# Transformer layer with routed experts: weight parts split by GpSimd within the attention, last shared block placed behind the expert tiles, padding rows copied at the end

## The reference

```
x = x + attn(layernorm(x))          # 16 query heads of 16, 4 key/value heads, causal softmax,
                                    # ternary weights for q, k, v and for the projection
h = layernorm(x)
scores = sigmoid(h @ w_router)      # 8 experts, the best 2 of each token, weights normalised
for e in range(8):
    he = silu(h @ w1[e]) * (h @ w3[e])              # 256 -> 176
    out = out + combine[:, e:e+1] * (he @ w2[e])    # 176 -> 256
shared = silu(h @ ws1) * (h @ ws3) @ ws2            # 256 -> 352 -> 256
x = x + out + shared
```

## Time and profile before

| | |
|---|---|
| median of 3 runs | 584.66 us (582.53 to 585.18) |
| profiled execution | 584.15 us, of which the span from the first to the last instruction is 582.2 us |
| mean granted TensorE clock | 0.915 of full speed |
| busy | TensorE 474.1 us, ScalarE 362.3, VectorE 313.5, GpSimd 170.9 |
| transfers | 61.36 MB, mean 105 GB/s |

### The profile page before, as it was taken

One profiled execution on the slowest core, in us unless ns is written; L12 is line 12 of the kernel. 1 busy time (PEld: TensorE's weight loads), 2 busy tenths in 40 slices (PEclk: granted clock), 3 DMA queues, 4 the chain that ended last, 5 costly groups with the idle time before them and its releaser, 6 DMA issues.

```text
span 582.2 us, 9830 instructions
## 1 busy us (share of the span) xinstructions
PE 474.1 (81%) x3202; PEld 264.9 (45%) x3202; DVE 313.5 (54%) x886; ACT 362.3 (62%) x567; POOL 170.9 (29%) x222
## 2 busy tenths in 40 slices
PE   1694869999999999999398768859797889999930
PEld 1582323233333333333143424327675789998920
DVE  6973516834713156131276555535957567666726
ACT  4255759989999989998369556615242335555520
POOL 3721101011110220103241172044455824444430
PEclk9878969999999999999599987868899989999985
DMA  8111012963999469243521022211011434444349
GB/s 207 31 48 41 11 32 86 301 163 98 289 296 282 112 48 4 1 92 98 145 55 57 2 74 86 62 43 56 28 57 40 124 74 119 124 117 125 110 138 340
DMA packets 77525, 61.36 MB, mean 105 GB/s; under 512 B 26984, under 2 KB 70600, under 8 KB 77480
## 3 DMA queue, kind: packets, MB, share of 16 engines
q1 hardware_dynamic: 73784, 51.04, 36.7%
q0 software_dynamic: 3408, 9.34, 4.5%
q10 hardware_dynamic: 288, 0.39, 0.2%
HBM read 19.88 MB, written 29.34 MB: 85 GB/s over the span
## 4 chain that ended last, share of the span: by engine, by line
PE 48%; DVE 18%; issue 14%; DMA 5%; POOL 5%; ACT 5%; SPq 4%; another core or an unknown queue 1%; DVEq 0%; ACTq 0%; POOLq 0%
PE ps L1575 16%; PE ps L1555 10%; PE ps L1747 6%; ACT prob L783 4%; PE ps L1765 3%; POOL rows_by_expert L658 2%; SPq L369 2%; PE ps L1584 2%; PE ps L1495 2%; DVE sm L922 2%; DMA yfin<-pair_out 2%; DVE sm L921 2%; PE ps L1769 1%; POOL hid_lo L687 1%; PE ps L1516 1%
## 5 line engine op out<-in xcount | busy, mean ns | idle before, releaser
L783 ACT ACTIVATE prob<-ps 128x1024 f32<-128x1024 f32 (+3 forms) x320 | 260.1, 919 | 70.6 <-PE ps L1555 68.6
L1575 PE MATMUL ps<-prob,v_sb 128*32 128x512 f32 (+3 forms) x1280 | 158.3, 569 | 18.3 <-DVE o_sb L1073 9.6
L1555 PE MATMUL ps<-qk 64*128 64x512 f32 (+3 forms) x640 | 121.1, 442 | 20.4 <-DMA qk<-qT 12.3
L617 POOL TENSOR_SCALAR_AFFINE_SELECT prob<-prob 128x512 f32<-128x512 f32 x64 | 41.3, 647 | 228.3 <-ACT prob L783 227.3
L1555 PEld LDWEIGHTS ps<-qk 64*128 64x128 f32 x640 | 54.1, 192 | 114.5 <-ACT prob L783 82.2
L1575 PEld LDWEIGHTS ps<-prob,v_sb 128*32 128x32 f32 x1280 | 26.0, 110 | 64.7 <-issue 34.0
L719 POOL DMA_INDIRECT pair_out<-yo,xg x39 | 37.5, 963 | 54.7 <-DVE yo L1431 54.4
L1073 DVE COPY o_sb<-ps 128x512 f32<-128x512 f32 x16 | 11.1, 691 | 65.2 <-PE ps L1575 64.6
L1693 PE MATMUL ps<-x2T,ws_hi 128*128 128x512 f32 (+1 forms) x96 | 33.0, 427 | 4.4 <-DVE hid L1300 4.4
L658 POOL DMA_INDIRECT rows_by_expert<-xs,slots x32 | 31.4, 981 | 14.2 <-issue 8.7
L1060 DVE CAST qT<-ps 96x512 fp32r<-96x512 f32 x16 | 11.0, 686 | 36.8 <-PE ps L1516 36.8
(11 more groups left out here) (203 smaller groups left out, 782.0 us busy)
## 6 DMA issues: line engine op xcount, KB each, us to landing
rows_by_expert<-pads SPq DMA_DIRECT2D x9, 1935.0 KB, 19.8
qk<-qT SPq DMA_DIRECT2D x138, 64.0 KB, 2.1
xg<-rows_by_expert SPq DMA_DIRECT2D x39, 129.0 KB
yfin<-pair_out SPq DMA_DIRECT2D x8, 512.0 KB, 7.3
stage<-in_w SPq DMA_DIRECT2D x8, 352.0 KB
x_sb<-in_x SPq DMA_DIRECT2D x4, 512.0 KB, 7.3
qk<-shT SPq DMA_DIRECT2D x8, 256.0 KB, 4.8
res<-in_x SPq DMA_DIRECT2D x4, 512.0 KB, 4.2
```

Of the source, the lines that this page charges most:

```text
L617: nc.gpsimd.affine_select(out=t, in_=t, compare_op=ALU.is_ge, fill=0.0, base=0, pattern=[[0, HPG], [1, P]], channel_multiplier=-1).then_in ...
L783: nc.scalar.activation(prob[:, u % NPB, 2 * hf:2 * hf + 2, c0:CH], ps[:, b:b + 2, c0:CH], ACT.Exp, scale=SCALE).then_inc(exp_done, 1)
L1555: ins = M(ps[:, 2 * (n % NSB) + h, c0:CH], qk[rows, par, PAIRS, kt * P:(kt + 1) * P], qk[rows, par, hf, j * CH + c0:(j + 1) * CH], start=T ...
L1575: ins = M(ps[VW * h:VW * (h + 1), O_BANK, c0:CH], v_sb[:, kt, :], prob[:, u % NPB, h, c0:CH], start=(kt == 0), stop=(u == LAST_OF[j]), ski ...
```

## The change

- Raw pieces are loaded during groups 0 to 2 into `NRAW` = 3 buffers, and GpSimd makes both parts into `NSPLIT` = 3 buffers, between masks in groups 1 and 2 (`SPLIT_AT`: behind unit 3, 11 and 23, 2 to 5 pieces at a place). SyncE stores the parts to DRAM and loads them back whole in the last group (`ws`, `ws2`, `w13`) and behind it (`w2_parts`). `high_piece` and `low_piece` are gone. The GpSimd loop over groups is written out.
- An expert's segment has 128 rows more (`SEG`). Only one block of 15 x 128 padding rows is written in DRAM (`pads_d`); when the last place is known, SyncE copies 128 of them behind each expert's last row (8 copies at run-time rows), and waits for these before it loads tiles.
- The last shared block's `up(11)` and `down(9..11)` are issued behind the tiles; its eviction stands between the second and the third of the four final additions.
- `hid_lo` of units 4 to 11 is made by VectorE; VectorE's order in the shared stage changes (`choose(2)` behind `scale_x2(3)`, `take_shared(1)` behind `list_tiles`), steps of `AFTER` move, step (4, 2) goes from unit 37 to 39.
- In group 0 round 1 is turned before the attention, rounds 2 and 3 one and two units earlier, and the scores of units 4 and 5 come behind the product of unit 3.

```diff
-SHARED_PIECES, EARLY_PIECES, POOL_PIECES = KD + 1, 9, 15
...
-NST = 2
-RES_AFTER = {4: 1, 7: 2, 8: 3}
+NRAW, NSPLIT = 3, 3
...
-    0: [("round", 0, 1)], 4: [("out", 0, 0)], 8: [("round", 0, 2)], 12: [("out", 0, 1)], 16: [("round", 0, 3)],
+    7: [("round", 0, 2)], 8: [("out", 0, 0)], 12: [("out", 0, 1)], 14: [("round", 0, 3)],
...
-    (0, 0): [("out", 0, 3), ("step", 5, 2)], (1, 0): [("step", 6, 2), ("step", 0, 3), ("step", 1, 3)],
-    (2, 0): [("step", 2, 3)], (2, 1): [("step", 3, 3)], (3, 0): [("step", 7, 2)],
-    (5, 0): [("step", 4, 3), ("step", 5, 3)], (6, 0): [("step", 6, 3)], (7, 1): [("step", 7, 3)],
+    (0, 0): [("out", 0, 3), ("step", 5, 2)], (1, 0): [("step", 0, 3), ("step", 1, 3), ("step", 6, 2)],
+    (2, 0): [("step", 2, 3), ("step", 3, 3)], (4, 0): [("step", 4, 3), ("step", 5, 3)],
+    (5, 0): [("step", 7, 2), ("step", 6, 3)], (6, 1): [("step", 7, 3)],
...
-LATE_PIECE_AT = {1: 9, 2: 10, 3: 11, 4: 12, 5: 13, 6: 14, 8: 15, 9: 16, 11: 17, 12: 18}
 EXP_AT = {19: 0, 31: 1}
-EXP_AFTER = {1: 2, 6: 3}
-LOW_PIECES = {3: range(0, 3), 11: range(3, 5), 23: range(5, EARLY_PIECES)}
+SPLIT_AT = {(1, 3): 2, (1, 11): 4, (1, 23): 3, (2, 3): 2, (2, 11): 5, (2, 23): 3}
+FLAT_FIRST = (NC - 1) * SH
+LOW_ON_DVE = range(4, FLAT)
...
+            def load_raw(n):
+
+                if n >= NRAW:
+                    sp.wait_ge(split_done, n - NRAW + 1)
+                for r, at, shape, src, _ in pieces_of(n):
+                    sp.dma_start(shaped(raw[0:r, n % NRAW, at:at + size_of(shape)], shape), src
+                                 ).then_inc(ld_raw[n % NRAW], 16)
+
+            def store_parts(n):
+
+                sp.wait_ge(split_done, n + 1)
+                for r, at, shape, _, to in pieces_of(n):
+                    for part in range(2):
+                        sp.dma_start(to[part], shaped(parts_f[0:r, n % NSPLIT, part, at:at + size_of(shape)], shape)
+                                     ).then_inc(st_parts[n % NSPLIT], 16)
+
+            def next_pieces(n0, n1):
+
+                for n in range(n0, n1):
+                    store_parts(n)
+                    if n + NRAW < len(PIECES):
+                        load_raw(n + NRAW)
...
+            for n in range(NRAW):
+                load_raw(n)
             sp.wait_ge(consts, CONSTS)
-            clear_rows(0, 3)
+            sp.dma_start(pads_d.rearrange("(k p) c -> p k c", p=P), pads[:].broadcast_to([P, PADS, ROW])).then_inc(zeroed, 16)
             for c in range(NC):
                 move(1, c)
-            sp.wait_ge(s_ready, 2 * NU)
-            clear_rows(3, blocks)
+            sp.wait_ge(zeroed, 16)
+            sp.dma_start(pads_d[:, ID:ID + 1].rearrange("(k p) c -> p k c", p=P), pad_ids[:].bitcast(F32),
+                         allow_slow_non_contiguous=True).then_inc(padded, 16)
+            next_pieces(0, 6)
             for c in range(NC):
                 move(2, c)
-            sp.wait_ge(zeroed, 16 * blocks)
-            for b in range(blocks):
-                sp.dma_start(rows_d[b * PADS * P:(b + 1) * PADS * P, ID:ID + 1].rearrange("(k p) c -> p k c", p=P),
-                             pad_ids[:, b * PADS:(b + 1) * PADS, :].bitcast(F32),
-                             allow_slow_non_contiguous=True).then_inc(padded, 16)
+            next_pieces(6, 9)
+            sp.wait_ge(padded, 16)
+            sp.dma_start(rows_d[E * SEG:ROWS, :], pads_d[E * P:PADS * P, :]).then_inc(padded, 16)
+            next_pieces(9, 16)
             for c in range(NC):
                 move(3, c)
+            next_pieces(16, len(PIECES))
+            for b in range(NSPLIT):
+                sp.wait_ge(st_parts[b], parts_stored(max(range(b, len(PIECES), NSPLIT))))
...
+            sp.dma_start(ws[:].bitcast(F32), ws_d).then_inc(ld_ws, 16)
+            sp.dma_start(ws2[:].bitcast(F32)[:, :, 0:SH - 1], ws2_d[:, :, 0:SH - 1]).then_inc(ld_ws, 16)
...
+            sp.wait_ge(x_free, step_use(3, 0))
+            sp.dma_start(res[:], x_t[:, TPC:2 * TPC, :]).then_inc(ld_res, 16)
+            for part in range(2):
+                sp.dma_start(w13[:, part].bitcast(F32), w13_d[:, part]).then_inc(ld_w13, 16)
+            for j in range(2, NC):
+                sp.wait_ge(x_free, step_use(3, j - 1))
+                sp.dma_start(res[:], x_t[:, j * TPC:(j + 1) * TPC, :]).then_inc(ld_res, 16)
+            sp.wait_ge(pv_done, NPB + NU * NKV)
+            sp.dma_start(w2_parts[0:FH].bitcast(F32), w2_d).then_inc(ld_w2, 16)
+
+            sp.wait_ge(ends_ready, 1)
+            for e in range(E):
+                end = nc.sync.value_load(ends[0:1, e:e + 1], min_val=e * SEG, max_val=e * SEG + T)
+                sp.dma_start(rows_d[bass.ds(end, P), :], pads_d[e * P:(e + 1) * P, :]).then_inc(padded, 16)
             sp.wait_ge(rows_ready, 1)
+            sp.wait_ge(padded, 16 * (2 + E))
...
+            def split_piece(n):
+
+                pool.wait_ge(ld_raw[n % NRAW], raw_loaded(n))
+                if n >= NSPLIT:
+                    pool.wait_ge(st_parts[n % NSPLIT], parts_stored(n - NSPLIT))
+                for r, at, shape, _, _ in pieces_of(n):
+                    a, hi, lo = (t[0:r, at:at + size_of(shape)] for t in (
+                        raw[:, n % NRAW], parts[:, n % NSPLIT, 0], parts[:, n % NSPLIT, 1]))
+                    nc.gpsimd.tensor_copy(hi, a).then_inc(split_step, 1)
+                    taken["n"] += 1
+                    pool.wait_ge(split_step, taken["n"])
+                    ins = nc.gpsimd.tensor_tensor(lo, a, hi.bitcast(F32), ALU.subtract)
+                ins.then_inc(split_done, 1)
+
+            taken = {"n": 0}
+            n = 0
+            for g in range(NKV - 1):
                 for u in range(NU):
                     if on_diagonal(u):
                         mask(g, u)
+                    for _ in range(SPLIT_AT.get((g, u), 0)):
+                        split_piece(n)
+                        n += 1
+            assert n == len(PIECES)
...
+            for n in range(LOW_ON_DVE[0]):
+                hidden_low(n)
...
+            rotate(TPC, 2 * TPC)
             dve.wait_ge(qkv_ready, NT)
             values(0)
-            rotate(TPC, 2 * TPC)
+            take_round(0, 1)
             squares_qk(0, 2 * TPC, NT)
-            for c in range(1, NC):
-                take_round(0, c)
-                if c == 1:
-                    copy_output(0, 0)
-                    scale_qk(0, 2 * TPC, NT)
-                    take_output(0, 0)
-                if c == 2:
-                    output(0, 1)
-                if c < NC - 1:
-                    rotate(TPC * (c + 1), TPC * (c + 2))
+            copy_output(0, 0)
+            scale_qk(0, 2 * TPC, NT)
+            rotate(2 * TPC, 3 * TPC)
+            take_round(0, 2)
+            take_output(0, 0)
+            rotate(3 * TPC, NT)
+            output(0, 1)
+            take_round(0, 3)
...
-            logits(2)
             low_part(0, 3)
             low_part(1, 3)
             rms_scale(3)
-            choose(2)
+            logits(2)
             hidden(1)
             add_residual(2, 3)
             add_residual(3, 3)
             hidden(2)
             row_stats(3, LN)
             scale_x2(3)
-            place(2)
+            choose(2)
             hidden(3)
-            take_shared(0)
-            hidden(4)
             low_part(4, 3)
             low_part(5, 3)
+            hidden(4)
+            place(2)
+            logits(3)
+            hidden_low(4)
+            take_shared(0)
             hidden(5)
-            logits(3)
+            choose(3)
+            hidden_low(5)
             hidden(6)
-            choose(3)
+            place(3)
+            hidden_low(6)
+            hidden(7)
+            list_tiles()
             take_shared(1)
-            hidden(7)
-            place(3)
+            hidden_low(7)
             hidden(8)
-            list_tiles()
+            hidden_low(8)
             hidden(9)
-            dve.wait_ge(piece_done, POOL_PIECES)
-            low_piece(15)
+            hidden_low(9)
             hidden(10)
-            take_shared(2)
-            low_piece(16)
-            hidden(11)
-            low_piece(17)
-            low_piece(18)
+            hidden_low(10)
...
+            hidden(FLAT - 1)
+            hidden_low(FLAT - 1)
+            finish(0)
+            finish(1)
+            take_shared(NC - 1)
+            dve.wait_ge(evicted, NC)
+            finish(2)
+            finish(3)
...
+                    if isinstance(g, int) and g == 0 and TPC <= u < TPC + LAG:
+                        pass
+                    elif u < NU:
                         scores(g, u, (g + 1) % 2)
                     elif following:
                         scores(g + 1, u - NU, g % 2)
                     times_values(g, q)
                     exchange(g, schedule, q, parts_next)
+                    if isinstance(g, int) and g == 0 and q == TPC - 1:
+                        for u in range(TPC, TPC + LAG):
+                            scores(g, u, 1)
...
```

(11 more changed lines are left out.)

268 lines of the change are left out of this document (110 added, 158 removed).

## The result

The kernel takes 565.12 us (median of 4 runs, 561.08 to 565.98) where the kernel before takes 584.92 (582.53 to 585.58): ratio 0.9663, 95% interval 0.9624 to 0.9702. In a second series beside the kernel before, the ratio was 0.9674 (0.9608 to 0.9741). It is clearly faster, by 3.4% where 5.4% was forecast, and the time lies just above the upper end of the range, 565. The profiled execution took 565.76 us, 1.76 more than its span of 564.0. The kernel before took 580.9, 576.8, 582.4, 582.1 and 578.2 in the later series, so that kernels of different series are compared by their ratios, and by stages.

A forecast was written before the change was run, and what follows sets the result against it. Weight pieces were taken to cost mainly by where they stand in VectorE's and GpSimd's in-order queues, making TensorE wait. 584.15 - 4.0 + 6.0 - 22.8 - 11.0 + 0.7 = 553.05, predicted 553 us, range 542 to 565.

The forecast's parts named there:

- Part 1: First attention group: earlier exchange rounds and reordered scores shorten the waits for keys, -4.0 us (bounds 0 and -8).
- Round 2 is queued one unit earlier, 1.7 us: First group: turning round 2 one unit earlier saves one unit's time, 69.0/40 = 1.7 us.
- Part 2: Middle groups, splitting on GpSimd, +6: late mask in the third group +4, VectorE held up in the second +2.
- Part 3: Last group: no weight pieces left in VectorE's or GpSimd's queue, -22.8 us (bounds -17 and -26).
- Both holes: Last group: TensorE's 8.32 us wait for the output copy and 8.51 us for a mask go, -8.3 and -8.5.
- The other short waits of that group ... stay: Last group: TensorE's remaining short waits, from chains within the routing, stay as they are.
- what is late next is the residual load: Last group: `res` lands some 7 us later behind SyncE's stores; costed at nothing, +3 if it slips.
- Part 4: Shared stage: moved block -7.1, waits -10.3, 6.4 put back; -11.0 us (bounds -7 and -19).
- second output block: Shared stage: TensorE must newly wait for its eviction behind the tile list, part of the 6.4 us put back.
- not on the path: Shared stage: eight padding copies at 0.88 us, 7.1 us beside the sends, cost nothing; if not, +4.
- Part 5: The end: moved block hidden under scatter and loads, its eviction enters VectorE's final sequence, +0.7 us (bounds +0.3 and +7.1).
- SyncE late: Rival: bursts wait for raw data or stores, padding copies or residual hold the routing; 566 us, chance 0.20.

The follow-up runs named there:

- e2: The changed kernel with round 2 of the first group turned behind unit 5 instead of unit 7; ratio 0.9611 to the kernel before, first group 81.9 us.
- e4: The changed kernel with GpSimd's four pieces behind unit 11 of group 1 held until VectorE has copied the output bank; no ratio, group 1 70.5 us.
- e1: The changed kernel with group 2's two pieces behind unit 3 moved to group 1 behind unit 23, raw data loaded earlier; ratio 0.9648 to the kernel before.
- the second profile: The changed kernel run once more, unchanged, in a later series; ratio 0.9674 to the kernel before.
- e8: The changed kernel with the last up block and last three down blocks put back ahead of the tiles; 564.97 us, ratio 0.9748 to the kernel before.
- e6: The changed kernel with the turn of block 2's normalised rows (first half) moved behind the first shared up block; 560.53 us, ratio 0.9712 to the kernel before.
- e7: The changed kernel with VectorE evicting the first shared block before the fifth hidden block, the second before listing tiles; no ratio, shared stage 63.0 us.
- e16: The changed kernel with the splitting placed anew and round 2 of the first group turned behind unit 4; 541.17 us, ratio 0.937 to the kernel before.
- e17: The edit of e7 on the changed kernel, run again with its ratio; 0.9516 to the kernel before, shared stage 62.8 us.
- e18: The edits of e16 and e7, plus block 2's turn moved and the last attention output ahead of it; 536.05 us, ratio 0.9264 to the kernel before.
- e14: The changed kernel with both shared evictions earlier and four of eight padding copies on ScalarE's queue; ratio 0.9718 to the kernel before, shared stage 73.0 us.

## Why the prediction was right and wrong

It is off by 12.7 us against its own execution (553.05 and 565.76): 5.1 in the last group, 3.2 in the middle groups, 2.6 in the tiles, 2.3 in the first group.

**Part 1, -4, measured -1.7.** The first wait ended at 54.63 as forecast. The step that failed is "Round 2 is queued one unit earlier, 1.7 us": the turn came 2.1 us earlier and not 3.3, and its transfers landed 0.4 later, so that the second wait ended 1.7 us earlier, no more than the first. From the end of the first wait to the turn it took 12.4 us where the kernel before took 12.7 with one unit more. A wait of 4.94 us was left of 6.89, although VectorE stood 8.52 us ready for that turn. The third wait was 0.42 us in the trace, not 0.7. e2 shows what two more units are worth there: 4.5.

**Part 2, +6, measured +9.2.** The mechanism was right to the place and nearly to the microsecond: raw piece at 215.0 (215.24), mask at 220.2 (221.06), TensorE waiting at unit 8 of the third group. The price was undersized, and this is the term that failed: 4.79 us of waiting plus some 2 behind it at half clock, +6.9 for +4. The +2 of the second group measured 2.3 in this profile and 0.8 in three others with the same wait of 1.1 us and no half clock behind it; e4 shows the cause of the wait. What I had not seen is that the third group had the same cause under the first one, which e1 uncovered.

**Part 3, -22.8, measured -17.7.** Both holes went. Two terms of the sum failed. "The other short waits of that group ... stay" and "what is late next is the residual load" had the wrong wait: late next was VectorE's chain to `xs`, for which TensorE waits 4.8 us in the group where it had waited 1.5, since the second hole had covered it; one of these waits is 3.3 or 3.4 us in every profile with that order. In all, TensorE's idle time fell by 14.7 us where 16.8 stood in the sum. And the half clock was put at -3.0 behind each hole, -6.0: TensorE's busy time fell by 3.0 only (90.6 to 87.6). The stretches behind the holes went, but others came or grew, and one, behind the wait for `xs`, fell into the first shared product, 4.59 us for 2.79. This term isn't firm: in the second profile the busy time was 83.4. ScalarE's unexplained wait (3.91) is no part of it, since the kernel before has it too (4.22). In the fourteen other runs that leave this group alone it took 94.7 to 102.4 us, median 98.4; but the 120.4 of before, from which the forecast starts, is one profile too, with that wait in it, and beside the five that have it as well (100.1 to 102.4) the forecast is 2.5 to 5 us too low.

**Part 4, -11.0, measured -11.1**, partly by luck. TensorE's busy time fell by 8.4 us where 7.1 stood in the sum, its idle time by 2.8 for 3.9. The moved block was worth 7.8 us net in e8 for 6.4. The waits for `hid`, `hid_hi` and `hid_lo` went almost wholly, and in their place came 4.6 us for the two evictions and 3.1 for the first rows. The first is the "second output block" that I had named, and the first block beside it. The second comes with the padding copies, which I had said were not on the path, for +4 if they were. Their 0.88 us each were taken from loads on an idle queue: in e6, e7, e8, e16, e17 and e18, without the stretches of the last section, eight took 9.5 to 9.9 us, 1.2 each, and in e6, e8 and e16, with the evictions as in the change, TensorE waited for no rows. So "not on the path" held there and failed in the profile of the change, whose copies took 13.28.

**Part 5, +0.7, measured +0.5** (24.38 from the last tile product for 23.88). The tiles' 2.6 us are not in the sum; in the other eighteen profiles they took 85.3 to 88.8 us, so that most of it is scatter of single profiles.

So the largest error is in the last group, then the middle groups, the tiles and the first group, and none was balanced by an overstated cost. In the second profile it lies otherwise: first group 84.9, middle groups 8.0 over those before, last group 98.4, shared stage 72.5. The rival "SyncE late", 566, gives the right time with other sums: it had +14 in the middle groups and -6 in the shared stage, and neither was measured.

## What to carry to other kernels

When a long wait is taken away, look on every engine for what it had covered, in the kernel before: how long each queue had stood ready at that moment, and what chain ended during the wait. The length of the work that is given to an idle engine may cost nothing; its price is where it stands: in which in-order queue, behind which data, beside which operations of another engine (VectorE's product took 0.42 us alone, 0.95 and 1.48 beside a difference of GpSimd). The same nineteen pieces cost 8 to 9 us at one set of places and none at another. For a wait of TensorE add the stretch at half clock that may follow: none or 1.5 us behind the same wait of 1.1 us, some 2 to 3 behind the longer ones. And before a difference of some us is put down to an edit, compare the stage in profiles that leave it alone.

## What had not been expected of the hardware

In three of five series, VectorE, ScalarE, TensorE and SyncE stood for 3 to 12 us, in large part together, with nothing in the trace that ended it, while GpSimd issued its sends of rows at 1.28 us each and up to 3 us beyond; so they did, more briefly, in the profiles of the kernel before and of the change with which the forecast is compared. In the other two series nothing of it was seen for the same instructions, and the kernel before was somewhat faster there too (576.8 and 578.2 us for 580.9 to 582.4). It isn't the chip alone: the second and the fourth series have the same chip number on record, the one without and the other with them. The padding copies came 1.26 us apart without such a stretch (9.5 us for eight) and up to 6 us apart with one. The records of instruction transfers don't fit it: the nearest one in e14 is near 442.5, after the engines had gone on at 441.1. What causes it stays open.
